# A float32 LoRA feed-forward kernel: batch 0's second product taken for both token tiles block by block, and w_up's low part made in place on VectorE

## The reference

```
y      = x[b] @ weight[ids[b]].T                    # 256 x 1024, per-batch adapter (1 of 8)
base   = y @ W_up.T                                 # the same W_up for all batches
top1   = argmax(y @ gate_w.T + expert_bias)         # one of 4 experts per token
z      = y @ lora_A[e].T   for all 4 experts        # rank 8 each: 32 columns
delta  = z[top1] @ lora_B[top1].T                   # only the chosen expert's part
out[b] = x[b] + base + delta
```

## Time and profile before

| what | value |
|---|---|
| median of 3 runs | 398.24 us (397.61 to 399.97) |
| span of the profiled execution | 397.9 us (the page has no other time of it) |
| PE matmul busy | 379.4 us, 95% |
| DVE busy | 213.9 us, 54% |
| ACT busy | 145.4 us, 37% |
| POOL busy | 17.5 us, 4% |
| mean granted clock of PE | 0.991 |
| HBM read, written | 55.20 MB, 8.39 MB |

### The profile page before, as it was taken

How to read it: one execution, slowest core, us unless ns; L and a number is a source line. 1 busy time by engine, 2 the same in 40 slices (tenths; PEclk the granted TensorE clock), 3 DMA queues, 4 the chain that set the end, 5 groups by cost and what they waited for, 6 DMA issues and landing times.

```text
span 397.9 us, 6753 instructions
## 1 busy us (share of the span) xinstructions
PE 379.4 (95%) x2240; PEld 355.0 (89%) x2240; DVE 213.9 (54%) x484; ACT 145.4 (37%) x316; POOL 17.5 (4%) x17
## 2 busy tenths in 40 slices
PE   2899869999999999999999999999999999999996
PEld 2689759889998999889998899988999899988996
DVE  3768495645546347456366455473573553654132
ACT  4766620637015340356105470153503452053100
POOL 0007520000000000000000000000000000000000
PEclk9999988999999999999999999999999999999999
DMA  6897856652096322971257611864229712450002
GB/s 187 300 360 224 261 216 190 239 203 82 24 285 202 146 105 84 273 230 45 105 137 283 213 50 55 248 225 160 105 60 267 234 71 105 146 170 0 0 0 105
DMA packets 21365, 63.65 MB, mean 160 GB/s; under 512 B 2544, under 2 KB 3696, under 8 KB 21360
## 3 DMA queue, kind: packets, MB, share of 16 engines
q1 hardware_dynamic: 21072, 63.07, 47.8%
q10 hardware_dynamic: 288, 0.52, 0.4%
HBM read 55.20 MB, written 8.39 MB: 160 GB/s over the span
## 4 chain that ended last, share of the span: by engine, by line
PE 87%; DMA 4%; DVE 4%; ACT 2%; SPq 1%; issue 1%; POOL 1%; ACTq 0%
PE ps_o L461 31%; PE ps_y L450 28%; PE ps_y L452 14%; PE ps_o L470 13%; PE ps_o L485 2%; DMA w_raw<-w_dram 2%; DMA lb_raw<-lora_b_dram 2%; DVE w_lo L346 2%; DVE x_hilo L339 1%; ACT up_hi L280 1%; POOL up_lo L244 1%; PE ps_y L478 0%; SPq L133 0%; SPq L149 0%; SPq L197 0%
## 5 line engine op out<-in xcount | busy, mean ns | idle before, releaser
L450 PE MATMUL ps_y<-x_hilo,w_hi 128*128 128x512 f32 x512 | 180.3, 397 | 9.4 <-DVE w_lo L346 7.8
L452 PE MATMUL ps_y<-x_hilo,w_lo 128*128 128x256 f32 x512 | 142.7, 279 | 0.0
L450 PEld LDWEIGHTS ps_y<-x_hilo,w_hi 128*128 128x128 f32 x512 | 96.8, 189 | 32.7 <-issue 7.4
L452 PEld LDWEIGHTS ps_y<-x_hilo,w_lo 128*128 128x128 f32 x512 | 97.0, 189 | 0.0
L346 DVE TENSOR_TENSOR w_lo<-w_raw,w_hi 128x512 fp32r<-128x512 f32 x128 | 81.4, 686 | 3.5 <-ACT w_hi L276 1.3
L461 PE MATMUL ps_o<-up_hi,y_hi 128*128 128x366 f32 x256 | 75.9, 337 | 1.9 <-POOL up_lo L244 1.9
L461 PE MATMUL ps_o<-up_lo,y_hi 128*128 128x366 f32 x256 | 74.8, 333 | 0.0
L461 PE MATMUL ps_o<-up_hi,y_lo 128*128 128x366 f32 x256 | 74.8, 333 | 0.0
L276 ACT CAST w_hi<-w_raw 128x512 fp32r<-128x512 f32 x128 | 71.3, 621 | 2.3 <-DMA w_raw<-w_dram 2.1
L296 ACT COPY y_small<-ps_y 128x256 f32<-128x256 f32 x64 | 23.8, 372 | 121.4 <-PE ps_y L452 121.4
L396 DVE TENSOR_TENSOR y_full<-ps_y,y_small 128x256 f32<-128x256 f32 x64 | 27.1, 424 | 68.8 <-ACT y_small L296 68.8
(11 more groups left out here) (33 smaller groups left out, 177.8 us busy)
## 6 DMA issues: line engine op xcount, KB each, us to landing
w_raw<-w_dram SPq DMA_DIRECT2D x63, 512.0 KB, 4.1
rows<-x_dram SPq DMA_DIRECT2D x16, 512.0 KB, 5.3
x_raw<-xT_dram SPq DMA_DIRECT2D x30, 256.0 KB, 7.0
up_raw<-w_up_dram SPq DMA_DIRECT2D x8, 512.0 KB, 6.7
out_dram<-rows SPq DMA_DIRECT2D x8, 512.0 KB, 7.7
out_dram<-rows SPq DMA_DIRECT2D x8, 329.0 KB, 7.2
out_dram<-rows SPq DMA_DIRECT2D x8, 183.0 KB, 6.7
x_raw<-xT_dram ACTq DMA_DIRECT2D x2, 256.0 KB, 3.4
```

The costliest lines, as they stand in the source:

```text
L450: pe.matmul(ps_y[c % 2][:, :], w_hi[:, c % RING, cols], x_hilo[:, k, :], start=(k == 0), stop=False)
L452: last = pe.matmul(ps_y[c % 2][:, S:2 * S], w_lo[:, c % RING, cols], x_hilo[:, k, 0:S], start=False, stop=(k == KC - 1))
```

## The change

It has five parts. (1) PE's batch 0 is written out ahead of the loop, and in its second product each block of w_up is used for tile 0 (banks a, b, c) and for bank c of tile 1 before the next block; then come bank b and bank a of tile 1, the two transposes within bank a, and all six lora matmuls at the end. (2) `up_raw` has eight slots, and `up_lo` is written over it (same addresses, in place); DVE makes all eight. (3) After each of y blocks 4 to 7 one up tile is split, and the other four alternate with the four x tiles of batch 1. (4) lora_b is split after the x tiles, its low part in one DVE operation over 64 partitions; for that the order of the four groups of 32 columns in `z_parts` is hi, lo, hi, lo. (5) SP issues gl and up tiles 0 to 3 among the w tiles 4 to 7, and waits for no slot of up_raw.

```diff
-    UP_AFTER = {4: (0, 1), 5: (2, 3), 6: (4, 5), 7: (6, 7)}
+    UP_EARLY = OC // 2
...
+        def sb_over(first, second, shape):
+            at = place(shape)
+            return (nc.alloc_sbuf_tensor_at(first, shape, F32, offset=at),
+                    nc.alloc_sbuf_tensor_at(second, shape, F32R, offset=at))
...
-        up_raw = sb("up_raw", [P, RING, H])
         up_hi = sb("up_hi", [P, OC, NW], F32R)
-        up_lo = sb("up_lo", [P, OC, H], F32R)
+        up_raw, up_lo = sb_over("up_raw", "up_lo", [P, OC, H])
...
             def load_up(c):
-                if c >= RING:
-
-                    sp.wait_ge(up_ready[c % 2], (c - RING) // 2 + 1)
-                sp.dma_start(up_raw[:, c % RING, :], w_up[c, :, :]).then_inc(up_raw_in[c % RING], 16)
+                sp.dma_start(up_raw[:, c, :], w_up[c, :, :]).then_inc(up_raw_in[c], 16)
...
-            for c in range(1, OC):
+            for c in range(1, RING):
                 load_w(0, c, i)
             sp.dma_start(gl_raw[:, :, :], gl[:, :, :]).then_inc(gl_in, 16)
-            for c in range(RING):
+            for c in range(RING, OC):
+                load_up(c - RING)
+                load_w(0, c, i)
+            for c in range(RING, OC):
                 load_up(c)
             for q in range(XQ):
                 load_x(1, q)
-            for c in range(RING, OC):
-                load_up(c)
...
-            for c in range(1, OC, 2):
-                pool.wait_ge(up_hi_ready, c + 1)
-                pool.tensor_tensor(up_lo[:, c, :], up_raw[:, c % RING, :], up_hi[:, c, 0:H].bitcast(F32),
-                                   ALU.subtract).then_inc(up_ready[1], 1)
...
-                        for u in UP_AFTER.get(c, ()):
-                            up_hi_part(u)
-                if first:
-                    lora_b_hi()
+                        if c >= UP_EARLY:
+                            up_hi_part(c - UP_EARLY)
                 if not last:
                     for q in range(XQ):
+                        if first:
+                            up_hi_part(UP_EARLY + q)
                         x_hi(b + 1, q)
+                    if first:
+                        lora_b_hi()
...
+            def lora_b_lo():
+                dve.wait_ge(lb_hi_ready, 1)
+                dve.tensor_tensor(lb_parts[2 * ER:P, :], lb_raw[2 * ER:P, :], lb_parts[2 * ER:P, :].bitcast(F32),
+                                  ALU.subtract).then_inc(lb_ready, 1)
...
-                    if first:
-                        for u in UP_AFTER.get(c, ()):
-                            if u % 2 == 0:
-                                up_lo_part(u)
+                    if first and c >= UP_EARLY:
+                        up_lo_part(c - UP_EARLY)
                 if not last:
                     for q in range(XQ):
+                        if first:
+                            up_lo_part(UP_EARLY + q)
                         x_lo(b + 1, q)
+                    if first:
+                        lora_b_lo()
...
+            def first_batch():
+                first_product(0)
+                pe.wait_ge(gl_ready, 1)
+                for c in range(OC):
+                    pe.wait_ge(up_ready, c + 1)
+                    pe.wait_ge(y_ready, c + 1)
+                    bank_ab(0, c)
+                    bank_c(0, c)
+                    bank_c(1, c)
+                for c in range(OC):
+                    bank_ab(1, c, (1,))
+                pe.wait_ge(eye_ready, 1)
+                for c in range(OC):
+                    if c == OC // 4:
+                        transpose_z(0, 0)
+                    if c == OC * 3 // 4:
+                        transpose_z(0, 1)
+                    bank_ab(1, c, (0,))
+                pe.wait_ge(lb_ready, 1)
+                for t in range(T):
+                    pe.wait_ge(zt_ready, t + 1)
+                    for k in range(3) if t == 0 else LAST:
+                        add_lora(t, k)
...
+            first_batch()
+            with nc.Fori(1, B, engines=(mybir.EngineType.PE,), hint_back_edge=True) as b:
+                batch(b)
```

More of the change, by code:

```diff
@@ L51, in build, with place @@
     with ExitStack() as ctx:
-        def sb(name, shape, dt=F32):
-            return ctx.enter_context(nc.sbuf_tensor(name, shape, dt))
+        spot = (nc.sbuf_base + 31) // 32 * 32
+        def place(shape):
+            nonlocal spot
+            at, n = spot, 4
+            for d in shape[1:]:
+                n *= d
+            spot += (n + 31) // 32 * 32
+            assert spot <= nc.sbuf_top, (spot, nc.sbuf_top)
+            return at
+        def sb(name, shape, dt=F32):
+            return nc.alloc_sbuf_tensor_at(name, shape, dt, offset=place(shape))
+        def sb_over(first, second, shape):
+            at = place(shape)
+            return (nc.alloc_sbuf_tensor_at(first, shape, F32, offset=at),
+                    nc.alloc_sbuf_tensor_at(second, shape, F32R, offset=at))
         def sem(name):
@@ L93, in build @@
         w_raw_in = [sem(f"w_raw_in{s}") for s in range(RING)]
-        up_raw_in = [sem(f"up_raw_in{s}") for s in range(RING)]
+        up_raw_in = [sem(f"up_raw_in{c}") for c in range(OC)]
         rows_in = [sem(f"rows_in{t}") for t in range(T)]
@@ L278, in up_hi_part @@
             def up_hi_part(c):
-                act.wait_ge(up_raw_in[c % RING], (c // RING + 1) * 16)
-                act.copy(up_hi[:, c, 0:H], up_raw[:, c % RING, :]).then_inc(up_hi_ready, 1)
+                act.wait_ge(up_raw_in[c], 16)
+                act.copy(up_hi[:, c, 0:H], up_raw[:, c, :]).then_inc(up_hi_ready, 1)
             def gate_hi():
@@ L350, in up_lo_part @@
                 dve.wait_ge(up_hi_ready, c + 1)
-                dve.tensor_tensor(up_lo[:, c, :], up_raw[:, c % RING, :],
-                                  up_hi[:, c, 0:H].bitcast(F32), ALU.subtract).then_inc(up_ready[0], 1)
+                dve.tensor_tensor(up_lo[:, c, :], up_raw[:, c, :],
+                                  up_hi[:, c, 0:H].bitcast(F32), ALU.subtract).then_inc(up_ready, 1)
+            def lora_b_lo():
+                dve.wait_ge(lb_hi_ready, 1)
+                dve.tensor_tensor(lb_parts[2 * ER:P, :], lb_raw[2 * ER:P, :], lb_parts[2 * ER:P, :].bitcast(F32),
+                                  ALU.subtract).then_inc(lb_ready, 1)
             def choose(b, t):
@@ L376, in choose @@
                 twice = zm[:, t, :].unsqueeze(1).to_broadcast([P, 2, ER])
-                hi = z_parts[:, t, 0:2 * ER].rearrange("p (k n) -> p k n", k=2)
-                lo = z_parts[:, t, 2 * ER:].rearrange("p (k n) -> p k n", k=2)
+                quads = z_parts[:, t, :].rearrange("p (k j n) -> p k j n", k=2, j=2)
+                hi, lo = quads[:, :, 0, :], quads[:, :, 1, :]
                 link(8, dve.tensor_copy(hi, twice))
@@ L486, in add_lora, with batch @@
                           start=False, stop=True, skip_group_check=(k == 2)).then_inc(out_done, 1)
-            with nc.Fori(0, B, engines=(mybir.EngineType.PE,), hint_back_edge=True) as b:
-                first_product(b)
+            def first_batch():
+                first_product(0)
                 pe.wait_ge(gl_ready, 1)
                 for c in range(OC):
-                    pe.wait_ge(up_ready[c % 2], c // 2 + 1)
+                    pe.wait_ge(up_ready, c + 1)
[17 more added lines that the diff above has]
+                        add_lora(t, k)
+            def batch(b):
+                first_product(b)
+                for c in range(OC):
                     pe.wait_ge(y_ready, b * OC + c + 1)
```

15 lines of the change are left out of this document (2 added, 13 removed).

## The result

The changed kernel takes **392.67 us** (median of 4 executions, 392.10 to 393.04) beside 398.73 us for the kernel before (4 executions, 397.61 to 399.97): ratio 0.9847, 95% interval 0.9820 to 0.9874, so 1.5% faster. The forecast was 390.2 us with a range of 389.2 to 393.0 us. The profiled execution has a span of 390.6 us and a time of 393.04 us.

What follows compares the result with a forecast made beforehand. TensorE was taken as the bound, busy 379.4 of 397.9 us, with the gain in batch 0's output product. 397.9 - 8.58 + 0.4 + 0.2 = 389.9 us span, plus 0.3 gives 390.2 us; range 389.2 to 393.0 us.

Steps and rivals of the forecast that it cites:

- Output product, -8.58 us: Batch 0's second product: waits for `up_lo` and `z_parts` and the low clock after them all go, saving 8.58 us.
- The time around the span, 0.3 us: Whole run: measured time taken as 0.3 us above the span, from the median of three runs.
- Rival 1: Batch 0's first product starves as w tiles queue behind up and gl: 3.2 us late, 393.0 us; chance 0.13.
- rival 3: PE's entry into the loop costs one instruction fetch, 1.8 us once: 392.0 us; chance 0.04.
- Loads, +0.4 us: Batch 0's first product: gl and up loads delay w tile 4, so PE's block 3 starts 0.4 us late.
- `up_lo` tight at block 3, +0.2 us: Batch 0's output product: `up_lo` 3 ready at 40.3 us, wanted at 40.5 us; 0.2 us allowed.
- `choose` and transposes, spare 3 us: End of batch 0: both `choose` end 2.9 and 3.0 us before PE reaches its transposes, so no wait.
- The end of batch 0, free: DVE adds six lora results in a row, 2.7 us, before the next `y_full` can start: no cost.
- the loop's entry, 0: PE enters the loop of seven with its sequencer 1.3 us ahead: no cost.
- rival 4: An instruction fetch comes at every loop turn, making the kernel slower, 428 us at 8.2 us each; chance 0.03.
- Rivals 1 and 2: First product starves, 393.0 us, chance 0.13; or the output product's `up_lo` wait stays, 391 to 396.6 us, chance 0.07.

Runs made afterwards that it cites:

- peeled kernel: Kernel before with only PE's batch 0 written out ahead of a loop over the other seven, in the old order: 399.18 us, ratio 1.0015.
- experiment 3: Changed kernel with gl and the first four up tiles issued behind w tile 7, as before the change: 391.23 us, ratio 0.9820.
- new end: Changed kernel with transposes before blocks 0 and 2 of bank a, five lora matmuls before block 5, one last: 391.64 us, ratio 0.9829.
- GpSimd kept busy: Changed kernel with four GpSimd subtractions on scratch tiles added, which nothing waits for: 397.57 us, one execution.
- The old order: Changed kernel with PE's batch 0 in the old order, tile 0 over all blocks, then bank c of tile 1: 393.52 us, ratio 0.9878.
- changed kernel's second trace: Changed kernel unaltered, run once more in a later set: 392.41 us, ratio 0.9852.
- lora_b later: Kernel before with ACT's lora_b cast moved behind batch 1's x tiles, low part still on GpSimd: 398.62 us, ratio 1.0011.

## Why the prediction was right, and which terms were off

**Output product, -8.58 us: right, for the execution it was read from.** In the two profiled executions it is 33.09 to 24.53 us, or 32.93 to 24.53 measured from the same matmuls, so 0.16 us of the term was batch 1's. Both waits went, as said. But 2.8 us of it are time in which PE is busy longer than a batch later; the peeled kernel has 0.5 us of that with the clock at 1.00, so some 2.2 us are the low clock's, and how much of it an execution has differs. The 47 executions of the kernel before in the three sets have spans from 394.2 to 398.4 us, median 396.6; the profiled one, with 397.9, was among the long ones. One of the 47 has a mean clock of 1.0 (the 394.2 us), 27 have 0.993 to 0.996 and 19 have 0.987 to 0.991, as the profiled one; the medians of the last two groups, 396.5 and 396.9 us, lie only 0.4 us apart, so the clock accounts for a small part of the 1.3 us by which the profiled execution is above the median, and the rest is open (the slow start of experiment 3, which no mean clock shows, can be in it). Of the gain that I forecast by span, 8.0 us, these 1.3 us are this one execution; measured by medians it is 6.1 us (396.6 to 390.5). The peeled kernel's trace shows the other kind of execution: a `z_parts` wait of 3.5 us with the clock at 1.00 behind it, and an output product of 28.58 us.

**The time around the span, 0.3 us: this is the term that was mis-sized.** The forecast's own band was 389.2 to 391.6 us, and 392.67 us lies above it; it is inside the stated range only by the part that was added for rivals 1 and 3, and neither happened. That much is luck. I set the span of one execution against the median of others. Each run's time is above its own span by about 1.8 us for the kernel before, and by 1.8 to 3.0 us (median 2.1 in the first four) for the changed one. Of the 2.5 us between 390.2 and 392.67 us it is 1.8. The other 0.7 is span, 390.6 against 389.9: 0.8 more than forecast in the first product and 0.4 in batch 1's, less 0.2 for the output product and 0.2 for PE's earlier first matmul (7.26 instead of 7.45 us). (Rounded, these add up to 0.8.) In relative terms the forecast of 2.0% became 1.5%.

**Loads, +0.4 us: right in its mechanism, but the first product was 0.8 us longer than that.** The landings of w tiles 4 and 5 came to 0.1 us. The wait that I had worked out for PE's block 3 shows as 0.25 and 0.28 us where PE keeps its pace (new end; GpSimd kept busy). In the profiled execution after, PE was behind it anyway: its second block ran at 1.2 GHz (clock 0.53 in 14 to 17.5 us) after 1.44 us of idle time before 12.7 us and 0.35 before 14 us, where the kernel before, after 1.19 and 0.32 us, kept full speed. So block 2 began 0.75 us late, and the pairs of batch 0 took 0.353 us instead of 0.347. With 0.2 us for PE's earlier start that makes 28.1 us instead of 27.0; 0.4 had been put. Moving the loads gave back 0.6 to 1 us. What makes one execution run that block slowly and another not, no run shows.

**`up_lo` tight at block 3, +0.2 us: right.** `up_lo` 3 was ready at 40.3 us, as worked out, and PE, which began 0.6 us later than thought, wanted it at 41.1. No wait. The old order, which wants a block every 1.46 us, waited 1.06 us.

**`choose` and transposes, spare 3 us: right.** `choose` began at 50.95 us (50.1 plus the 0.6 us by which PE came late) and PE reached its transposes at 55.74 and 57.86 us, 2.8 and 2.9 us after `z_parts` was made.

**The end of batch 0, free; the loop's entry, 0: half wrong.** Six results took 2.61 us on DVE and nobody waited. The lead at the entry was 1.5 us (1.3 worked out) and no gap appeared, so rival 3 and rival 4 did not happen: the changed kernel's loop turns show no gap either. But batch 1's first product cost 0.4 us more in another way, which none of the rivals had. The forecast had named a section of the Trainium skill (Runtime: NRT & Kernel Launch, "Instruction fetch mechanics") against this part. It speaks of taken branches, and at the loop's entry none is taken: the loop's line has its first compare-and-branch at 104.2 us, 2.9 us ahead of the first product of batch 2.

```profile
L545 PEldq COMPARE_BRANCH  x7: 88/228/248, 104.2 to 384.4; - x7
```

At the turns, where a branch is taken, no trace here shows a gap; whether a fetch hides in that lead can't be told from them. Rival 3 was thus a case that the entry does not have.

**Rivals 1 and 2** did not happen. Rival 1's end, 393.0 us, lies near the result, and even its sign came, a first product above 28 us (28.1). But its mechanism did not: the landings were 2.5 to 2.6 us apart, not 3.5, and PE did not wait at block 3. The sign was a poor one, since a slow block of PE gives it as well.

## What to carry to other kernels

Before a wait is costed, take the clock behind it apart from the wait itself, and look how far single executions differ: what a low clock adds is not the same every time, and a gain read from one execution can be too large. Measure the time around the span on the same execution as the span. When one row of an engine stands for several operations, take them one by one: four x subtractions in 6.92 us were two of 0.7 and two of 2.9 us. Then look at who works beside the long ones before looking at the queue: an "idle" helper engine can cost more than it takes over. Reordering the cause (lora_b later) did nothing; taking it off GpSimd did most.

## What was not expected of the hardware

- The same y product ran at 0.353 or at 0.347 us per pair of matmuls, 22.60 or 22.20 us in all, with the clock at 1.00 in both. In batch 1 it followed the lead of PE's sequencer at the start of the product (1.5 us or 3.0 us) in all thirteen traces. In batch 0 both paces occur as well (0.353 in the peeled kernel, 0.347 in the kernel before), and in the changed kernel's second trace it goes from 0.353 to 0.347 within the product, at 22 us, in block 3. What sets it there is open.
- A GpSimd operation of 32 partitions by 1024 holds up the one two-input subtraction of VectorE that it meets until it has finished itself: by 1.7 us where the GpSimd operation had 1.8 us left, by 2.2 us where it had 2.35 us left, and the same for a subtraction of 0.69 us as for one of 1.22.
- The kernel before ran with a mean clock anywhere between 0.987 and 1.0. A `z_parts` wait of 3.7 us was followed by half clock in its trace and with lora_b later, one of 3.5 us by none in the peeled kernel's.
- PE's first matmuls run at half pace in every trace, until 10.7 us in some and 17.3 us in others, and the granted clock on the page reads 1.00 for it.
